# Cross attention in a decoder kernel: in odd units the side product goes ahead of the scores and the products with the values

## The reference

```python
qh = jnp.einsum('bld,hde->hble', q, w_q)          # 16 heads of 64
kh = jnp.einsum('bld,hde->hble', k, w_k)
vh = jnp.einsum('bld,hde->hble', v, w_v)
scores = jnp.einsum('hbqe,hbke->hbqk', qh, kh) * scale
scores = jnp.where(mask[None], -jnp.inf, scores)
attn = jax.nn.softmax(scores, axis=-1)
out = jnp.einsum('hbqk,hbke->hbqe', attn, vh)
...
out = out @ w_o + b_o
x = out + residual
return _layer_norm(x, gamma, beta)
```

## Time and profile before

| | |
|---|---|
| median of 3 runs | 2763.75 us (2757.05 to 2773.28) |
| profiled execution | 2759.56 us |
| its span | 2757.8 us |
| TensorE busy | 2457.9 us (89%) |
| VectorE busy | 1752.8 us (64%) |
| ScalarE busy | 1356.7 us (49%) |
| GpSimd busy | 1149.9 us (42%) |
| TensorE's granted clock, mean | 0.961 of full speed |

### The profile page before, as it was taken

How to read it: one execution, slowest core, us unless ns; L and a number is a source line. 1 busy time by engine, 2 the same in 40 slices (tenths; PEclk the granted TensorE clock), 3 DMA queues, 4 the chain that set the end, 5 groups by cost and what they waited for, 6 DMA issues and landing times. The chain is left out here.

```text
span 2757.8 us, 47258 instructions
## 1 busy us (share of the span) xinstructions
PE 2457.9 (89%) x18594; PEld 1493.3 (54%) x18594; DVE 1752.8 (64%) x3198; ACT 1356.7 (49%) x2386; POOL 1149.9 (42%) x612
## 2 busy tenths in 40 slices
PE   5989999999997769999998799999979888788899
PEld 2334434344343324454545588999945555577657
DVE  2799989998999847787777541111236666466433
ACT  4566565666655336667675431111246666232331
POOL 2789889988889813434343201222220000200030
PEclk8999999999999989999999999999989999899999
DMA  5031230311304063444344235555320000200030
GB/s 220 1 130 38 86 138 1 122 70 69 123 9 160 0 178 68 93 88 96 71 83 114 49 126 189 180 186 178 105 74 1 1 1 1 92 9 1 1 109 31
DMA packets 126108, 227.21 MB, mean 82 GB/s; under 512 B 7904, under 2 KB 97504, under 8 KB 109760
## 3 DMA queue, kind: packets, MB, share of 16 engines
q1 hardware_dynamic: 122144, 213.95, 24.8%
q0 software_dynamic: 3744, 10.23, 1.0%
HBM read 201.74 MB, written 22.41 MB: 81 GB/s over the span
## 5 line engine op out<-in xcount | busy, mean ns | idle before, releaser
L208 POOL TENSOR_TENSOR m_h<-m_h,m_bc 128x1024 f32<-128x1024 f32 x256 | 612.2, 2411 | 79.1 <-DVE m_h L521 79.1
L521 DVE TENSOR_TENSOR_SCAN m_h<-m_da,m_h 128x1024 f32<-128x1024 f32 x256 | 578.3, 2275 | 42.6 <-ACT m_da L411 42.5
L281 PE MATMUL m_psy<-m_h,m_ident 128*128 128x512 f32 x1024 | 492.8, 613 | 24.3 <-POOL m_h L208 24.3
L411 ACT ACTIVATE m_da<-x_rows,m_a_neg 128x511 f32<-128x511 f32 x512 | 330.7, 680 | 153.6 <-DVE m_h L521 150.3
L942 POOL TENSOR_SCALAR c_pr<-c_pr,c_share 128x512 f32<-128x512 f32 x128 | 200.0, 1563 | 374.6 <-DVE c_share L1224 374.6
L281 PEld LDWEIGHTS m_psy<-m_h,m_ident 128*128 128x128 f32 x1024 | 196.6, 197 | 292.1 <-issue 234.3
L508 DVE TENSOR_TENSOR m_h<-m_dtx,m_bc 128x1024 f32<-128x1024 f32 x192 | 231.7, 1207 | 24.4 <-PE m_psy L281 18.0
L227 PE MATMUL m_rot<-early_ctx,early_w 128*128 128x512 f32 x240 | 134.2, 688 | 60.5 <-ACT m_gz L387 42.1
L1107 ACT ACTIVATE c_pr<-c_pr,c_low 128x512 f32<-128x512 f32 x256 | 180.9, 707 | 3.6 <-DVE c_low L1216 3.5
L988 PE MATMUL c_psS<-c_kT,c_qT 64*128 64x512 f32 x512 | 147.1, 652 | 32.3 <-DVE c_low L1216 28.4
L1113 ACT ACTIVATE c_pr<-c_pr,c_share 128x512 f32<-128x512 f32 x128 | 92.3, 721 | 161.1 <-DVE c_share L1224 160.7
(11 more groups left out here) (396 smaller groups left out, 4019.1 us busy)
## 6 DMA issues: line engine op xcount, KB each, us to landing
m_bc<-bc_dram SPq DMA_DIRECT2D x32, 2048.0 KB, 8.9
e_up<-in_up SPq DMA_DIRECT2D x39, 1024.0 KB, 5.1
c_vr<-v_dram SPq DMA_DIRECT2D x128, 256.0 KB, 5.0
v_dram<-c_stage SPq DMA_DIRECT2D x32, 256.0 KB, 2.3
e_down<-in_down SPq DMA_DIRECT2D x8, 1024.0 KB, 12.6
e_down<-y_dram SPq DMA_DIRECT2D x8, 512.0 KB, 7.5
h_w<-in_w SPq DMA_DIRECT2D x2, 2048.0 KB, 14.8
m_taps<-in_taps SPq DMA_DIRECT2D x1, 2560.0 KB, 12.1
```

What stands on the lines that cost most here:

```text
L208: pool.tensor_tensor(hq, hq, bc[:, 1, NP * s:NP * (s + 1), :], ALU.mult).then_inc(p_ready, 1)
L281: mm = pe.matmul(bank, ident[:], h[:, n % HB, e, :], start=False, stop=(s == NG - 1 and e == NP - 1))
L411: ins = act.activation(da[:, n % 2, e, at:at + L - 1], dt[:, u, j, at:at + L - 1], ACT.Exp, scale=a_neg[:, u, j, NP * s + e:NP * s + e + 1])
L521: dve.tensor_tensor_scan(flat, decay, flat, 0.0, ALU.mult, ALU.add).then_inc(scanned, 1)
```

## The change

In odd units `extra(n)` is called at the head of the loop body, ahead of scores(n+2) and of the two calls of attend. In even units nothing moves.

```diff
                 for n in range(TOTAL + 8):
                     b, u = divmod(n, UNITS)
+                    if n in numbers and n % 2 == 1:
+                        extra(n)
                     if n + 2 < TOTAL:
                         needed(n + 2)
                         scores(n + 2)
                     if LT <= n < TOTAL + LT and n % 2 == 1:
                         attend(n // LT - 1, n % LT - 1)
                         attend(n // LT - 1, n % LT)
-                    if n in numbers:
+                    if n in numbers and n % 2 == 0:
                         extra(n)
```

## The result

The changed kernel took 2952.8 us (median of 4 runs, 2946.9 to 2957.5) against 2760.7 before: a ratio of 1.069, 95% interval 1.066 to 1.072. Forecast were 2935 us and a range of 2870 to 2990.

What follows compares the result with a forecast made beforehand. The prediction took PE to bound the kernel, busy for 89% of the span. Its terms 104.2+5.4+12.7+27.2+26.4 = 175.9 us, added to 2759.6, gave 2935 us, with a range of 2870 to 2990.

Steps and rivals of the forecast that it cites:

- The bound: Cross attention stage: PE, busy for over 90% of each of batches 0 to 2, sets the end.
- The projection pair, +104.2: 42 pairs: odd side product waits for ScalarE's copy, so a pair takes 10.45 instead of 7.97 us, +104.2 us.
- The picture of the pair: Changed PE timeline: a hole of 2.4 to 2.6 us before the odd side product, near 1.3 before the even one.
- Output pairs, +5.4: Six pairs, units 4 to 7: bank freed by a DVE add, 12.15 instead of 11.45 us plus about 0.2, +5.4 us.
- Transposing pairs, +12.7: Six pairs with a side product of only 0.59 us: each takes 9.13 us by the chain, +12.7 us together.
- What loses its cover, +27.2: DVE and ScalarE side work behind odd units delays the chain by 49.2 us, less 22 already paid: +27.2 us.
- The clock, +26.4: PE's clock falls behind long holes at some 16 places, 1.65 us each: +26.4 us, bounds 0 to 89.
- The length of a batch: Batches 1 and 2 of the changed kernel take some 190 to 200 us.
- only the bare wait: Rival, chance 0.13: side work slides into DVE's idle time and the clock holds, 2869 us.
- the clock in every pair: Rival, chance 0.06: PE's clock falls in every pair of the stage, 2998 us.
- not slower: Rival, chance 0.03: the next even side product finds its bank free and 22 us of small waits go, 2738 us.

Runs made afterwards that it cites:

- The bank of its own: Changed kernel, with odd units' side products (all but output products) in a separate bank taken from the scores: 2765.0 us, ratio 1.001.
- the early copy: Changed kernel, with ScalarE copying the side product between its scale and its exponentials instead of behind them: 2846.6 us, ratio 1.030.
- the moves to even units: Changed kernel with six layer norm parts on DVE (2925.7 us), square roots on ScalarE (2928.3 us), or both (2907.1 us) moved behind even units.
- The long filler: Changed kernel with small extra products in PE's holes, two to nine in holes lengthened by side work: 2926.1 us, ratio 1.059.
- long filler over short: Short means the changed kernel with only one or two small extra products ahead of each wait for the bank: 2942.1 us, ratio 1.065.

## Why the prediction was right, point by point

- **The bound.** Right: PE was idle for only 34.5 of the 415.2 us of batches 0 to 2 before, and the holes and slow products that the order made went straight into the span.
- **The projection pair, +104.2.** Right in mechanism and size: 10.44 measured, 10.45 worked out; X(o) at 5.40 to 5.53 after S(e), 5.45 worked out. The bank of its own shows that the wait is the whole of it, the early copy that its date is set by ScalarE's order.
- **The picture of the pair.** Wrong in a part that the sum doesn't use: I announced a hole of 2.4 to 2.6 us ahead of X(o) and one of 1.3 ahead of X(e), and so counted the second twice. In steady state X(e) starts 2.33 after S(e), and the holes are 1.19 and 1.10 (or 1.68 and 0.7). The choice that the clock holds in the steady pairs was argued from a bare gap of 2.48 us that never occurs in them; that it came out right is in part luck.
- **Output pairs, +5.4.** The mechanism held, the size was off: 12.3 to 12.6 and, in the first pair of each two, 13.8 to 13.9 (three of each: some 10 us). I had not carried ScalarE's late copy into the first of them.
- **Transposing pairs, +12.7.** Not tested by themselves. X is so short here that a root and x_apply fall into one hole, and the clock falls behind it each time. The twelve output and transposing pairs cost 32 us together; the terms of 18.1 leave out x_apply, the root and the clock in these pairs, which the sum had in its other terms.
- **What loses its cover, +27.2.** Right in mechanism, shown by the moves to even units; a root's 2.45 is seen to the hundredth in the timeline. The moves gave 27.1 and 24.5 us, against 17 and 15 for the delays alone. In these two traces the products of batches 0 to 2 are also 8.0 and 3.5 us shorter, so the delays by themselves were worth some 19 and 21, my estimate. That all side work is hidden behind even units holds for DVE's parts, not for every root.
- **The clock, +26.4.** Right that it falls behind the long holes and not in the steady pairs, too small in size. The long filler gave 26.7 us, but that isn't the whole price: the same products took 44.5 us longer in batches 0 to 2. I expected 16 falls at 1.65 us. In batches 0 to 2 alone the timeline has 23 places where a product turns slow behind a hole, at some 1.9 us each (44.5/23). I expected them behind holes of 4.4 to 4.9 us; most of those holes are 3.5 to 5.3, but eight falls came behind holes of 2.0 to 3.0 us and one behind 1.68.
- **Left out.** The last pair of batch 0 has no side product and was priced at nothing; it took 7.85 instead of 5.19 us, as the late chain ran into it. The pair at units 12 and 13 of batch 3 was priced like any projection pair, at 2.48; it took 16.6 instead of 13.2, 3.4 more.
- **The length of a batch.** Announced were 190 to 200 us for batches 1 and 2; they took 205.3 and 204.7.

The sum, 175.9, fell 16 us short of the measured 192. The clock's term is enough to explain it: it is up to 18 us too small in batches 0 to 2 alone. Their idle time grew by 132.6 us, and the other terms come to about 138 there (38 of the 42 projection pairs, four of the six output pairs). That the 26.4 of the term and the 26.7 of the filler agree is chance. The rivals: "only the bare wait" falls, since moving the side work alone gave 45.7 us back; "the clock in every pair" falls, since the seven steady pairs keep a granted clock of 1.00; "not slower" falls by the result.

## What to carry to other kernels

Two products into one accumulation bank must stand as far apart in the producer's order as the consumer takes to come to its copy, and that distance is counted in the consumer's whole instruction order, not in the 0.57 us of the copy. Work put between them is free cover; take it away and it is paid in full, and what is behind the waiting product (here the scores that feed everyone) is late as well and uncovers work on engines that look half idle. If such an order is wanted, give it a second bank or move the copy up first, and price the edit by following one steady pair from release to release.

## What the runs showed of the hardware that I had not expected

The length of a single hole doesn't tell whether TensorE's clock falls. In the changed kernel a product ran at half clock (1.2 GHz) behind 2.00 us of idle, with a hole of 1.22 us shortly ahead; the same product of the same pair (units 12 and 13) kept its full clock (2.4 GHz) behind 2.67 us in batch 1 and lost it behind 2.66 us in batch 2:

```profile
1059.08 3.63 PE L964 MATMUL carried<-x_cols,c_wq 128*128 128x512 f32 x4 [2.00 <-ACT c_kT L1095]
...
1285.38 1.98 PE L964 MATMUL carried<-early_w,c_ctxT 128*128 128x512 f32 x4 [2.67 <-ACT c_stage L1095]
...
1489.25 3.68 PE L964 MATMUL carried<-early_w,early_ctx 128*128 128x512 f32 x4 [2.66 <-ACT c_stage L1095]
```

The granted clock is 0.54 from 1059.0 to 1062.7, 1.00 from 1285.0 to 1287.4 and 0.56 from 1489.0 to 1492.9. The hole shortly ahead doesn't settle it either: it was 0.81 us where the clock held and 0.38 where it fell. What decides is open.

And filler products on the engine that bounds the stage paid: 16 us from long filler over short, at a granted clock of 0.98 instead of 0.93. The Trainium skill (TensorE: Matmul & The Clock Gate, section HAM oscillation — how this bites in real kernels) describes a clock that falls anew in each round of a loop with a wait in it. Here that is seen behind the long holes, and not in the rounds whose holes were 1.1 and 1.2 us, or 1.7 and 0.7.
